# A GRU layer between two feed-forward layers on one core: the base products spread over the odd steps, the experts' products behind them

## The reference

```
x = x + FFN0(LayerNorm(x + attention summary of x))      # gate, up, down; block-quantised operands
x = x + FFN1(GRU over the 256 positions of x)
```

```
gi = x_t @ W_ih + b_ih ;  gh = h @ W_hh + b_hh
r = sigmoid(i_r + h_r) ;  z = sigmoid(i_z + h_z) ;  n = tanh(i_n + r * h_n)
h = (1 - z) * n + z * h
```

## Time and profile before

| | |
|---|---|
| median of 3 runs | 1716.18 us |
| profiled execution | 1720.65 us, its span 1718.80 us |
| PE matmul busy | 1556.5 us, 91% of the span, 32268 instructions |
| DVE busy | 1393.3 us, 81% |
| ACT busy | 644.6 us, 38% |
| POOL busy | 497.5 us, 29% |
| waits for the state's low part hT (L759) by PE's state products | 44.1 us |
| mean granted TensorE clock | 0.96 of full |

### The profile page before, as it was taken

One profiled execution on the slowest core, in us unless ns is written; L12 is line 12 of the kernel. 1 busy time (PEld: TensorE's weight loads), 2 busy tenths in 40 slices (PEclk: granted clock), 3 DMA queues, 4 the chain that ended last, 5 costly groups with the idle time before them and its releaser, 6 DMA issues.

```text
span 1718.8 us, 75109 instructions
## 1 busy us (share of the span) xinstructions
PE 1556.5 (91%) x32268; PEld 1204.4 (70%) x32268; DVE 1393.3 (81%) x5571; ACT 644.6 (38%) x1624; POOL 497.5 (29%) x573
## 2 busy tenths in 40 slices
PE   5634689999999999999999999999999999999986
PEld 2321267777777777777777777787777777778874
DVE  6887788888888888888888888888888888887654
ACT  5566233333333333333333333333333333333331
POOL 6774322222222222222222222222222222211000
PEclk9866799999999999999999999999999999999997
DMA  6744221122221111122111111112111112221000
GB/s 239 270 153 134 56 45 43 40 49 49 46 49 38 35 46 46 48 47 49 44 45 49 49 46 49 32 38 49 46 46 49 49 43 46 49 43 37 25 16 20
DMA packets 122444, 101.01 MB, mean 59 GB/s; under 512 B 91904, under 2 KB 92288, under 8 KB 121728
## 3 DMA queue, kind: packets, MB, share of 16 engines
q1 hardware_dynamic: 121824, 96.02, 20.9%
q10 hardware_dynamic: 288, 0.19, 0.0%
HBM read 58.43 MB, written 16.78 MB: 44 GB/s over the span
## 4 chain that ended last, share of the span: by engine, by line
PE 76%; DVE 15%; issue 3%; ACT 2%; DMA 2%; POOL 2%; SPq 0%; DVEq 0%; ACTq 0%; POOLq 0%
PE ps_rn_turn L1312 24%; PE ps_gi L1212 12%; PE ps_z L1312 10%; PE ps_down L1179 6%; PE ps_gate_up L1170 6%; PE ps_base L1221 4%; PE ps_gate_up L1160 4%; PE ps_base L1264 3%; PE ps_route L1221 3%; DVE fe L821 1%; POOL qfT L1028 1%; DVE gi L630 1%; DVE gi L628 1%; PE ps_rn_turn L1200 1%; DVE zn L806 1%
## 5 line engine op out<-in xcount | busy, mean ns | idle before, releaser
L1312 PEld LDWEIGHTS ps_rn_turn<-hT,whh 128*128 128x128 f16 x16320 | 435.0, 96 | 83.7 <-DVE hT L759 70.2
L1312 PE MATMUL ps_rn_turn<-hT,whh 128*128 128x32 f16 x16320 | 449.3, 176 | 44.5 <-DVE hT L759 44.1
L1046 POOL TENSOR_TENSOR qf<-f8c,fe 128x512 bf16<-128x512 bf16 x128 | 134.3, 1049 | 873.0 <-DVE f8c L838 873.0
L1212 PEld LDWEIGHTS ps_gi<-x1T,wih 128*128 128x128 f16 x4608 | 274.5, 98 | 38.2 <-issue 3.8
L1212 PE MATMUL ps_gi<-x1T,wih 128*128 128x128 f16 x4608 | 290.2, 220 | 1.7 <-ACT gi L574 1.7
L583 ACT ACTIVATE r_tanh<-r_pre,scale_half 128x64 f32<-128x64 f32 x256 | 89.0, 348 | 525.1 <-DVE r_pre L779 525.1
L1312 PE MATMUL ps_z<-hT,whh 128*128 128x32 f16 x8160 | 243.3, 176 | 0.0
L1312 PEld LDWEIGHTS ps_z<-hT,whh 128*128 128x128 f16 x8160 | 222.7, 96 | 0.0
L574 ACT ACTIVATE gi<-ps_gi,b_i,scale_x 128x128 f32<-128x128 f32 x384 | 144.7, 457 | 190.9 <-PE ps_gi L1212 190.8
L773 DVE TENSOR_TENSOR r_half<-ps_rn_turn,gi 128x64 f32<-128x64 f32 x256 | 56.2, 220 | 127.8 <-PE ps_rn_turn L1312 123.6
L585 ACT ACTIVATE z_tanh<-z_pre,scale_half 128x64 f32<-128x64 f32 x256 | 89.0, 348 | 155.8 <-DVE z_pre L789 155.8
(11 more groups left out here) (201 smaller groups left out, 2403.8 us busy)
## 6 DMA issues: line engine op xcount, KB each, us to landing
wih<-in_x_steps SPq DMA_DIRECT2D x32, 256.0 KB, 5.8
xin<-in_x_steps SPq DMA_DIRECT2D x32, 256.0 KB, 2.9
xres<-in_x_steps SPq DMA_DIRECT2D x32, 256.0 KB, 3.0
x_dram<-x SPq DMA_DIRECT2D x32, 256.0 KB, 2.3
x_in_bias<-x_dram SPq DMA_DIRECT2D x32, 256.0 KB, 2.8
out_rows<-y SPq DMA_DIRECT2D x32, 256.0 KB, 2.0
stage<-in_ffn_w SPq DMA_DIRECT2D x12, 512.0 KB, 3.9
sg_gs<-in_ffn_w SPq DMA_DIRECT2D x12, 512.0 KB, 3.9
```

Of the source, the lines that this page charges most:

```text
L1046: g.tensor_tensor(blocked(qf[:, :]), blocked(f8c[:, :]), spread(fe16[:, :]), ALU.mult).then_inc(qf_done, 1)
L1212: last = mm(ps_gi[:, j * P:(j + 1) * P], wih_parts[:, k, at:at + P], x1T[:, x, k, :], start=k + w + x == 0, stop=k == KD - 1 and w == 1)
L1312: last = mm(ps[:, (at + j) * 2 * B:(at + j + 1) * 2 * B], whh[:, k, u, gate * D + j * P:gate * D + (j + 1) * P], hx(t)[:, 2 * k:2 * k + 2, ...
```

## The change

The four parts of the base product move to steps 1, 3, 5 and 7, one part in each, in all chunks with a recurrence. The two calls of `experts` move within step 7 from ahead of up to the end of the step's list, behind base part 3, since they add to what it completes. The table for the last chunk, without a recurrence, stays.

```diff
             x_parts = ((0, (0,)), (0, (1, 2, 3)), (1, (0, 1)), (1, (2, 3)), (2, (0, 1)), (2, (2, 3)))
-            base_parts = {4: (0,), 6: (1, 2, 3)}
+            base_parts = {1: (0,), 3: (1,), 5: (2,), 7: (3,)}
             base_parts_at_end = {0: (0,), 3: (1, 2, 3)}
@@ others
                 if E and s == 7:
                     spread_scale(e, L)
-                if L and s == 7:
-                    experts(l, 0)
-                    experts(l, 1)
                 if F:
                     (gate, up)[s % 2](f, s // 2)
@@
                 if L:
                     for k in (base_parts if R else base_parts_at_end).get(s, ()):
                         base(l, k)
+                if L and s == 7:
+                    experts(l, 0)
+                    experts(l, 1)
```

## The result

The changed kernel takes 1788.22 us (median, 1786.75 to 1789.52) against 1715.36 us before (four runs, 1712.65 to 1718.49): ratio 1.0426, 95% interval 1.0414 to 1.0438. It is slower, as forecast; 1788 lies within 1762 to 1800 and 9 us above the 1779 named. The profiled execution took 1786.75 us with a span of 1785.0 us, 66.2 us more than the span before.

The account below looks back on a forecast made before the run. Each step was taken to last until the later of TensorE's list and VectorE's state chain. Steps added 2.19 us a chunk, 63 us in all, giving 1784 profiled and 1779 us as median; range 1762 to 1800.

Parts of the forecast that it names:

- Odd steps: Steps 1, 3, 5 and 7 end on TensorE, so each grows by a whole base part, 0.65 us.
- changes nothing in this sum: Claim that moving the experts inside step 7 does not alter the odd steps' sum of 27.00 us.
- Steps 4 and 6: End on VectorE after losing base parts: step 4 stays 5.40 us, step 6 goes to 4.94, giving back 0.48.
- Step 0: y waits for the late experts and delays r_half on VectorE's queue: 6.04 us against 5.56, a loss of 0.48.
- not held by y: Rival: y does not delay step 0's first read, step 0 stays near 5.56 us; 1766 us, chance 0.08.
- Step 2: GpSimd's pair on xg ends earlier, so fe on VectorE shortens: 5.28 us against 5.68, a gain of 0.40.
- list of signs: Expected 0.4 wait before step 3; wrong if chunk below 47.5, step 6 over 5.2, step 0 under 5.7, many low-clock stretches.
- fe keeps its 0.88: Rival in step 2: 0.88 us is fe's own time, so the step stays 5.68; 1790 us, chance 0.07.
- The clock: Rival: waits in step 6 lower TensorE's clock in one chunk in three, 14 us more; 1793 us, chance 0.10.
- The sum: Steady chunk 48.66 us against 46.47, 2.19 slower; 59 us over 27 chunks, 63 with the last four.
- last chunks: Last four chunks, where stages drop out: two at full price, two at none, 4 us in all (bounds 0 and 9).
- Faster: Rival: only TensorE's total counts and all waits go, chunk 45.50 us; 1690 us, chance 0.02.

Follow-up runs that it names:

- e1: Kernel before, with only the experts' two calls moved behind everything in step 7; base parts stay in steps 4 and 6: 1726.48 us, ratio 1.0062.
- e5: Changed kernel, but base part 3 and the experts run ahead of up in step 7: 1767.70 us, ratio 1.0288 to the kernel before.
- e3: Changed kernel plus four unread bf16 matmuls at the end of TensorE's list in step 6: 1777.97 us, ratio 1.0361 to the kernel before.
- e4: Changed kernel plus two unread bf16 matmuls in step 4, none in step 6: 1789.88 us, ratio 1.0428 to the kernel before.
- e7: Kernel before, with VectorE's xn moved ahead of inter and fam in step 2: 1696.03 us, ratio 0.9879.

## Why the prediction was right, and where it was off

**What bounds the kernel** was read rightly. Comparing TensorE's list with VectorE's chain in each step gave seven of the eight lengths within 0.08 us and step 2 within 0.24, the chunk 48.66 against 48.41.

**Odd steps** grew by 0.65 each, as said (0.66, 0.65, 0.65). Step 7 grew by 0.57 only. The experts take 1.98 us behind the single small matmul of `spread_scale` and 1.88 behind another group of matmuls, in e1 as in e5; that tenth I had put at nothing ("changes nothing in this sum").

**Steps 4 and 6** stayed on VectorE: 5.42 and 4.98 against 5.40 and 4.94. e3 and e4 put work into both without lengthening them, so this is shown.

**Step 0** was forecast at 6.04 and is 6.05. e1 (only this edit: 6.05) and e5 (the rest of the change without it: 5.56) show from both sides that y behind the late experts is the cause. The rival "not held by y" falls.

**Step 2** is the term of the sum that was mis-sized: 5.04, not 5.28, a gain of 0.65 instead of 0.40, 6.5 us over 27 chunks. I had passed 0.25 us of step 1's later first read on to GpSimd. In the trace r_half of step 1 is late by 0.20 (2.01 against 1.81 after the start), yet the new state is written at 4.88, where it was 4.86: z_half had been waiting 0.19 us for TensorE, and that wait absorbed the delay. So GpSimd's pair ends 2.52 into step 2, not 2.76, and TensorE's wait before step 3 is 0.16 us, not the 0.4 of my list of signs. One reading in that paragraph was wrong too: xn isn't done "long before step 2 begins". It starts at 1035.93 in the trace before and ends 0.46 into step 2, behind inter and fam. The gain doesn't hang on this: all of these follow step 1's state on VectorE, so they come earlier against step 2 when TensorE makes step 1 longer. That fe is held by GpSimd's operation is shown by e7. By the Trainium skill (SBUF — State Buffer, Who interferes with whom) when VectorE runs in a two-port mode and GpSimd holds the port pair that they share, the one that issued second blocks until the other's instruction is done. The traces agree: fe ends 0.03 and 0.04 us after GpSimd's operation where they overlap, and takes 0.16 where they don't. Which mode fe runs in no run here shows. The rival in which fe keeps its 0.88 falls.

**The clock** was given 0.10 as a rival of its own, and it came, beside the forecast's mechanism rather than in its place. I had set it at nine stretches of 1.56 (14 us); it was eight, 12.1 us together, in chunks 1 to 27. That it was just one chunk in three was luck: nothing in the prediction works that out. The step that failed is the argument against it: that the stretch 1582 to 1622, as busy as the new chunk, kept 1.00. That was a share over 40 us. What the runs point to is more local: the changed kernel's slow stretches lie right behind a wait of 1.3 us and the state products, and filling the wait ends them (e3). The trace before had this too: its two slow stretches, in chunks 2 and 14, lie in step 3, behind the only wait of a steady chunk (1.16 and 0.89 us there). I saw such a row and did not draw that from it. Not every wait does it: e1 has the same wait before step 3 and no slow stretch. By my own list of signs, many slow stretches were to count against the forecast, and they do: its figure without the clock was too low.

**The sum.** Against the forecast span of 1781.8 the measured one is 1785.0: steps -7 (2.19 x 27 = 59 forecast, 52 measured), clock +9, last chunks +4 (8 instead of 4), preparation -3. The other 6 us of the 9 between 1779 and 1788 are the offset from profiled execution to median: I took 4.5 off, but the changed kernel's profiled execution lies 1.5 below its median. For the last chunks, where stages drop out, I took two at the full price and charged no clock, and a ninth slow stretch of 1.6 us lies in chunk 28; there are no experiments on these chunks, and their part is an account of the trace, not shown. That the forecast came within 9 us is partly luck: the steps came out 7 us and the preparation 3 us shorter than forecast, the clock took 9 us and the last chunks 4 us more, and the four nearly cancel.

**Faster** needed the even steps under 19.47 us together; they take 21.49.

## What to carry to other kernels

Where two engines hand a state to and fro, write down for each step when either is done; work is free only in steps where the engine that does it is the earlier one, and costs its full length in the others, so equal portions are not a balance. Look at what stands in the queue behind an instruction whose producer is moved later: nothing in the recurrence needed y's result, but r_half stood behind it in VectorE's queue. And a wait of the matmul engine can cost twice, once for itself and once through the clock of what comes next.

## What was not expected of the hardware

Four matmuls that nobody reads made a kernel 10 us faster (1777.97 against 1788.22). With waits of 1.33 us before the state products (matmuls of 32 columns, 2.5 us in all) TensorE's clock fell to 1.2 GHz in every third chunk, at distances of 146.8 us that held over eight chunks; with 0.47 us in that place it fell in none of 27 (one profiled execution of each). One small VectorE operation on 16 columns, held behind GpSimd, was worth more than the best placement of the base products tried: ratio 0.9879 against 0.9950.
